# Norm, gate and last norm of batches 0 and 1 inside the last slots of attention 1; projections 0 and 1 back to back

## What is computed

```
x = x + L0_attn(norm(x))                 # 8 heads of 32, window 64
x = x + L0_xattn(ctx, norm(x))           # state space scan over ctx, gated by silu(norm(x))
x = x + L0_ffn(norm(x))                  # 256 -> 704 -> 256
x = x + L1_attn(norm(x))                 # 16 query heads of 128, 4 key/value heads, causal
x = x + L1_xattn(ctx, norm(x))           # second scan over ctx, gated by silu(norm(x))
x = x + L1_ffn(norm(x))                  # shared expert + 6 of 32 experts by a router

def L1_attn(x):                          # per batch
    q, k, v = split(x @ w_qkv.T)
    q, k = norm(q) * g + b, norm(k) * g + b      # per head
    q, k = rope(q), rope(k)
    return softmax(causal(q @ k.T / sqrt(128))) @ v @ w_o.T

def xattn(ctx, z):                       # u, delta, B, C come from ctx alone
    state[t] = state[t-1] * exp(delta[t] * A) + delta[t] * u[t] * B[t]
    return (state[t] @ C[t] + D * u[t]) * silu(z)
```

## Time and profile before

| | us |
|---|---|
| median of 3 runs | 902.63 (901.39 to 903.73) |
| the profiled execution | 903.65 |
| its span, first to last instruction | 901.9 |

### The profile page before, as it was taken

How to read it: one execution, slowest core, us unless ns; L and a number is a source line. 1 busy time by engine, 2 the same in 40 slices (tenths; PEclk the granted TensorE clock), 3 DMA queues, 4 the chain that set the end, 5 groups by cost and what they waited for, 6 DMA issues and landing times.

```text
span 901.9 us, 12578 instructions
## 1 busy us (share of the span) xinstructions
PE 747.9 (83%) x4016; PEld 576.4 (64%) x4016; DVE 688.0 (76%) x1230; ACT 490.2 (54%) x1062; POOL 352.6 (39%) x247
## 2 busy tenths in 40 slices
PE   6660479877799993699999999999856799999997
PEld 2240356554433573577877787878744689999996
DVE  4897689889879887798899899899967554444443
ACT  1744458640336602477786877788833354444442
POOL 1001355452331544223332423333533286666663
PEclk9885669898899997799999999999977899999999
DMA  4341124235020212011111111211400243444431
GB/s 173 122 154 42 70 93 140 96 140 221 1 76 0 59 59 93 0 48 36 48 45 38 48 48 36 60 36 51 151 1 0 100 147 136 142 139 143 139 132 47
DMA packets 28886, 74.66 MB, mean 83 GB/s; under 512 B 3632, under 2 KB 6336, under 8 KB 28448
## 3 DMA queue, kind: packets, MB, share of 16 engines
q1 hardware_dynamic: 28384, 71.51, 23.2%
q10 hardware_dynamic: 448, 2.49, 0.8%
HBM read 72.55 MB, written 1.44 MB: 82 GB/s over the span
## 4 chain that ended last, share of the span: by engine, by line
PE 54%; DVE 18%; issue 13%; ACT 11%; POOL 3%; DMA 1%; POOLq 0%; DVEq 0%; ACTq 0%; SPq 0%
PE ps L1864 6%; PE ps L1865 6%; PE ps L1866 6%; PE ps L1829 4%; PE ps L1706 4%; DVE hS L1033 3%; PE ps L1817 3%; PE ps L1752 2%; PE ps L1751 2%; PE ps L1750 2%; PE ps L1799 2%; PE ps L1798 2%; PE ps L1510 2%; DVE ps L1025 2%; PE ps L1483 1%
## 5 line engine op out<-in xcount | busy, mean ns | idle before, releaser
L420 POOL TENSOR_TENSOR hS<-hS,BCb 128x512 f32<-128x512 f32 x64 | 81.6, 1279 | 140.2 <-issue 69.0
L1462 DVE SCALAR_TENSOR_TENSOR arena<-ps,arena 128x1024 f32<-128x1024 f32 x32 | 39.2, 1225 | 101.6 <-ACT arena L899 93.1
L443 POOL TENSOR_TENSOR hS<-hS,BCb 128x1024 f32<-128x1024 f32 x23 | 56.1, 2440 | 108.2 <-DVE ps L1025 94.1
L509 POOL TENSOR_TENSOR MHl<-arena,MHh 128x1024 fp32r<-128x1024 f32 x34 | 81.8, 2405 | 17.2 <-ACT MHh L902 17.1
L1491 PE MATMUL ps<-ident,hS 128*128 128x128 f32 x256 | 40.7, 316 | 54.9 <-POOL hS L443 48.5
L1864 PE MATMUL ps<-Wh,MHh 128*128 128x256 f32 x272 | 77.8, 286 | 5.3 <-POOL MHl L509 5.3
L1063 DVE TENSOR_TENSOR_SCAN hS<-dA,ps 128x512 f32<-128x512 f32 x64 | 78.1, 1221 | 2.8 <-DVE ps L1054 0.6
L1866 PE MATMUL ps<-Wh,MHl 128*128 128x256 f32 x272 | 77.7, 286 | 0.0
L1865 PE MATMUL ps<-Wl,MHh 128*128 128x256 f32 x272 | 77.6, 285 | 0.0
L1491 PEld LDWEIGHTS ps<-ident,hS 128*128 128x128 f32 x256 | 33.7, 162 | 65.4 <-POOL hS L443 54.9
L506 POOL TENSOR_TENSOR Wl<-WB,Wh 128x512 fp32r<-128x512 f32 x34 | 47.1, 1388 | 64.5 <-ACT Wh L883 64.5
(11 more groups left out here) (241 smaller groups left out, 2100.7 us busy)
## 6 DMA issues: line engine op xcount, KB each, us to landing
BCb<-bc_dram SPq DMA_DIRECT2D x32, 512.0 KB, 3.5
BCb<-bcq_dram SPq DMA_DIRECT2D x64, 256.0 KB, 3.2
arena<-gate_dram SPq DMA_DIRECT2D x32, 512.0 KB, 3.8
WB<-in_we SPq DMA_DIRECT2D x34, 256.0 KB, 2.6
WB<-in_wqkv SPq DMA_DIRECT2D x1, 3072.0 KB, 12.7
WA<-in_wo ACTq DMA_DIRECT2D x1, 2048.0 KB, 7.9
WA<-in_ffn SPq DMA_DIRECT2D x1, 1408.0 KB, 7.9
pkb<-in_pk SPq DMA_DIRECT2D x2, 698.0 KB, 4.7
```

Source lines behind the costliest of these rows:

```text
L420: gp.tensor_tensor(h, h, qbc(q)[:, 1:2, :].broadcast_to([P, DT, S]), ALU.mult).then_inc(s["c_ready"], 1)
L443: gp.tensor_tensor(h, h, BCb[g % SB_LOADS][:, 1:2, :].broadcast_to([P, DT, HALF]), ALU.mult).then_inc(s["c_ready"], 1)
L509: gp.tensor_tensor(MHl[:, p, :], MH[p], MHh[:, p, :].bitcast(F32), ALU.subtract).then_inc(s["m_lo"], 1)
```

## The change

**End of attention 1.** Norm 4, gate and norm 5 of half 0, with transposes, copies, and the high and low parts of the result, become pieces of the plan in slots 53 to 63 (`GATE1_FIRST_HALF`). Behind the plan the same steps stand for half 1 alone. The tanh of layer 1 goes to the arena instead of `hT`. The low part of half 0 stays on VectorE, in slot 63. Counts on semaphores follow the new order (`ln_count`, `x_count`). The planner counts the new pieces of VectorE.

**Start of attention 1.** `ln_apply(3, 1)` becomes the piece `apply1`, behind `rope` of job 0 and job 1. Jobs 0 and 1 have `rope` three and `tr` four slots behind `proj` instead of two and three; the square of job 1 no longer waits for the sum of job 0. The transposes of half 1 (`ln1`) go from slot -6 to -3, V of batch 0 from -5 to -1 (behind the first scores). `accq` of quarters 6 to 9 goes behind projection 1. `da` of quarters 10 to 12 goes from slot 0 to -5. On GpSimd `w1_low(3)` and `(4)` stand ahead of `ln_rstd(3, (1,))` and `(5)` behind it, without the wait for norm 3.

```diff
+        gate_scratch = lambda l, hf: ar(4 + 8 * hf, 1024) if l else hT[:, hf, :]
...
+        def x_count(L, t):
+
+            if L == 4:
+                return XN_FFN + t // 2 + 1 + (t // 2 == B - 1)
+            if L == 5:
+                return XN_FFN + B + 2 * (t // 4)
+            return XN[L] - 1 + t // 4
+
+        LATE_LNS = {(4, 0): 8, (5, 0): 9, (4, 1): 10, (5, 1): 11}
+        ln_count = lambda L, hf: LATE_LNS.get((L, hf), 2 * L + hf) + 1
...
+            w1_low(3)
+            w1_low(4)
             ln_rstd(3, (1,))
-            pool.wait_ge(s["ln_h"], NT * 4)
-            w1_low(3)
+            w1_low(5)
...
-                elif kind == "sum":
+                if kind == "ln4":
+                    ln_rstd(4, (0,))
+                elif kind == "gate_x":
+                    ln_rstd(5, (0,))
+                elif kind == "sum":
                     job(JOB[a])
-                    if JOB[a] < 2:
-                        w1_low(4 + JOB[a])
...
-            ln_rstd(4)
+            ln_rstd(4, (1,))
...
-            ln_rstd(5)
+            ln_rstd(5, (1,))
...
-                if j:
+                if j >= 2:
                     act.wait_ge(s["job_sum"], j)
...
+            def final_high(hf):
+                act.wait_ge(s["ln_tr_dve"], 6 + hf + 1)
+                act.wait_ge(s["ln_tr_act"], 6 + hf + 1)
+                z = slice(512 * hf, 512 * hf + 512)
+                sc.copy(hTh[:, :, z], hT[:, :, z]).then_inc(s["h_hi"], 1)
...
+                if kind == "ln4_apply":
+                    gate_tanh(1, (0,))
+                elif kind == "ln5_copy":
+                    ln_tr_copy(3, (0,))
+                elif kind == "final":
+                    final_high(0)
...
-            ln_tr_copy(3)
+            ln_tr_copy(3, (1,))
+            final_high(1)
...
-            ln_apply(3, 1)
...
+            def final_low(hf):
+                z = slice(HALF * hf, HALF * hf + HALF)
+                dve.wait_ge(s["h_hi"], hf + 1)
+                v.tensor_tensor(hTl[:, :, z], hT[:, :, z], hTh[:, :, z].bitcast(F32), ALU.subtract).then_inc(s["h_lo_dve"], 1)
+
             for kind, a in ATT1_PLAN:
+                if kind == "ln4":
+                    ln_stats(4, 0)
+                elif kind == "ln4_apply":
+                    dve.wait_ge(s["job_mm"], len(JOB))
+                    dve.wait_ge(s["v_mm"], B)
+                    ln_apply(4, 0)
+                elif kind == "gate_h":
+                    gate_h(1, 0)
+                elif kind == "gate_x":
+                    gate_x(1, 0)
+                elif kind == "ln5_apply":
+                    ln_apply(5, 0)
+                elif kind == "ln5_copy":
+                    ln_tr_copy(3, 0)
+                elif kind == "final_low":
+                    final_low(0)
+                elif kind == "rot":
                     job(*a)
+                elif kind == "apply1":
+                    ln_apply(3, 1)
...
-            for hf in both:
-                ln_stats(4, hf)
-            dve.wait_ge(s["job_mm"], len(JOB))
-            dve.wait_ge(s["v_mm"], B)
-            for hf in both:
-                ln_apply(4, hf)
-            gate(1)
-            for hf in both:
-                ln_apply(5, hf)
-            for hf in both:
-                ln_tr_copy(3, hf)
...
+            ln_stats(4, 1)
+            ln_apply(4, 1)
+            gate_h(1, 1)
+            gate_x(1, 1)
+            ln_apply(5, 1)
+            ln_tr_copy(3, 1)
...
+            def gate_tr(l, halves=(0, 1)):
+
+                if l:
+                    pe.wait_ge(s["job_tr_copied"], 2 * len(JOB))
+                for hf in halves:
...
             fd(1)
-            for q in step:
-                accq(q)
             ln_ready(2, 0)
...
+                elif kind == "gate_tr":
+                    gate_tr(1, (0,))
+                elif kind == "ln5_tr":
+                    ln_tr(3, (0,))
+            gate_tr(1, (1,))
+            ln_tr(3, (1,))
...
+GATE1_FIRST_HALF = [(53, "ln4"), (54, "ln4_apply"), (55, "gate_h"), (56, "gate_tr"), (57, "gate_x"), (59, "ln5_apply"), (60, "ln5_tr"),
+                    (61, "ln5_copy"), (62, "final"), (63, "final_low")]
...
-    rope_job(-8, 0, 0, 2, 3)
-    rope_job(-7, 0, 1, 2, 3)
+    rope_job(-8, 0, 0, 3, 4)
+    rope_job(-7, 0, 1, 3, 4)
     at(-7, "wo1", 0)
-    at(-6, "ln1", 0)
-    v_job(-5, 0)
+    for q in range(Q_IN_FFN - 4, Q_IN_FFN):
+        at(-7, "acc", q)
+    at(-4, "apply1", 0)
+    at(-3, "ln1", 0)
+    v_job(-1, 0)
...
+    for slot, kind in GATE1_FIRST_HALF:
+        at(slot, kind, 0)
-    cost = {"rot": 2.6, "sum": 1.2, "rope": 3.2, "step": 2.0}
-    ssm = [("da", (m, d)) for m in range(Q_IN_FFN, Q_IN_FFN + 3) for d in range(DT)]
+    cost = {"ln4": 1.7, "ln4_apply": 1.4, "gate_h": 1.2, "gate_x": 4.3, "ln5_apply": 1.4, "ln5_copy": 0.7, "final_low": 1.2, "rot": 2.6, "sum": 1.2, "rope": 3.2, "step": 2.0}
+    ssm = []
+    for m in range(Q_IN_FFN, Q_IN_FFN + 3):
+        for d in range(DT):
+            at(-5, "da", (m, d))
...
-        plan += pick("ln1", "v", "proj") + behind
+        plan += pick("ln1", "v", "proj", "acc") + behind
...
-        plan += pick("vc", "sq")
+        plan += pick("vc", "sq", "da")
         if ok(u - 1):
             plan += [("pt", u - 1), ("ptc", u - 1)]
+        plan += pick(*(kind for _, kind in GATE1_FIRST_HALF))
         plan += [p for p in now if p[0] == "da"]
-        plan += pick("wo1", "rope", "rot", "sum")
+        plan += pick("wo1", "rope", "apply1", "rot", "sum")
```

More of the change, by code:

```diff
@@ L878, in _ @@
                     yq_copy(a)
-            gate_tanh(1)
+            gate_tanh(1, (1,))
             def w_high(x, src):
@@ L1245, in _ @@
+            for hf in both:
+                gate_h(0, hf)
+            for hf in both:
+                gate_x(0, hf)
             for hf in both:
@@ L1681, in _ @@
             acc_to(LAYER_STEPS - 1)
-            def gate_tr(l):
-                for hf in range(2):
+            def gate_tr(l, halves=(0, 1)):
+                if l:
+                    pe.wait_ge(s["job_tr_copied"], 2 * len(JOB))
+                for hf in halves:
                     pe.wait_ge(s["gate_h"], 2 * l + hf + 1)
```

76 lines of the change are left out of this document (29 added, 47 removed).

## The result

The changed kernel takes 904.75 us (median of 20 executions, 901.53 to 908.29) against 901.67 for the kernel before, measured beside it: a ratio of 1.0037, 95% interval 1.0025 to 1.0049. It is slower by 0.4%; the forecast was 0.6% faster. Its profiled execution took 905.45 us with a span of 903.7 us, 1.8 us more than the span of before.

What follows compares the result with a forecast made beforehand. Engines waiting on each other bound start and tail, nearly full TensorE and VectorE attention. 903.65 - 4.8 (tail) - 4.5 (start, net) + 3.5 (attention) = 897.85 profiled, 896.8 us median; range 890.5 to 904.

Steps and rivals of the forecast that it cites:

- Which views bound what: Attention 1 by stretches: engines wait for each other at start and tail; TensorE and VectorE nearly full in the early slots.
- The tail: Behind attention, to the router's end: half 1 goes through alone, 7.6 off the chain, 2.8 onto it, 4.8 us less.
- The start: From the feed-forward's last residual to the first `rc`: waiting falls from 15.2 to 6.3 us, 8.9 us shorter.
- What it pays there: Ahead of the start, GpSimd's `w1_low(3)` and `(4)` hold tiles 3 and 4 of `ln_apply(3, 0)`: 4.4 us later.
- Attention itself: Slots 0 to 63: half 0's work moves five scan steps into earlier slots, 3.5 us more, bounds 0 and 14.
- the lateness is nearly covered. I take a fifth: Early slots: ScalarE's own `da` work nearly covers VectorE's lateness, so 2 of 10.3 us of extra steps show.
- My 1.2: Last eleven slots: 11.5 us of moved pieces come in, 10.3 of steps leave, so 1.2 us more VectorE work.
- A: Rival at layer 3's norm tiles: they slip ahead of `w1_low` or TensorE has slack, 4.4 less, 892.4 us; chance 0.22.
- B: Rival in attention: VectorE becomes the bound and lateness isn't caught up, 14 us against 9.3 gained, 907.3 us; chance 0.10.
- C: Rival in attention: all 10.3 us of extra steps show but the rest doesn't, 903.6 us; chance 0.15.
- D: Rival at the start: it keeps its length as another wait replaces the one removed, 901.3 us; chance 0.10.
- Signs to look for: Changed profile: first `rc` about 370.3, residual 335, first to last `rc` 285, tail 23.6; wrong if `rc` stretch grows over 6.

Runs made afterwards that it cites:

- even: Kernel before plus a VectorE sum over 112 columns that nobody waits for in each of the 64 slots: 902.71 us, ratio 1.0003.
- start_only: Kernel before with only the part of the change ahead of attention 1: 898.42 us, ratio 0.9966.
- start_gated: Kernel before with the start part alone, plus a GpSimd wait for all four norm tiles ahead of `w1_low(3)`: 891.34 us, ratio 0.9886.
- end_only: Kernel before with only the change's part in and behind the last slots, planner costs included: 908.78 us, ratio 1.0072.
- steps_only: start_gated with scan steps placed as in the changed kernel (44 early, 10 late) and no piece moved: 898.48 us, ratio 0.9962.
- dve_only: start_gated plus five VectorE sums of 1.95 us in slots 5, 18, 24, 34 and 40: 894.98 us, ratio 0.9930.
- all_parts: start_gated plus five times a step's work on TensorE, VectorE, ScalarE and GpSimd, without moving batch boundaries: 895.61 us, ratio 0.9935.
- whole: Changed kernel with the GpSimd wait, 39 steps in their old slots and the five displaced ones whole in slots 5, 18, 24, 34, 40: 896.23 us, ratio 0.9938.
- y_behind_sq: Changed kernel with the GpSimd wait and ScalarE's copy of `y` put behind the square of its slot: 896.64 us, ratio 0.9932.
- whole_apart: whole with the copy of `y` last in its slot on ScalarE and the next batch's first accumulation one slot later: 895.61 us, ratio 0.9925.
- late_fixed: start_gated with half 0's norm 4 statistics, norm and tanh taken behind slot 63, GpSimd's 1/sqrt behind its last product with C: 892.07 us, ratio 0.9889.

## Why the prediction was wrong, point by point

- **Which views bound what**: right as read, wrong as used. TensorE at 227.84 and VectorE at 221.50 of 240.26 were both named as nearly full; I then priced VectorE's lateness alone.
- **The tail**, 4.8 less (bounds 4 to 5.5): 4.3 from the last residual to the router's end. Confirmed. The mis-sized term is the router: 5.29 instead of 4.79, at a granted clock of 0.67 instead of 0.74. I had reckoned with the last copy and not with the clock. Another 0.7 ahead of the last residual (5.91 instead of 6.64) can't be put down to the change: even, which leaves this place alone, has 5.91 too.
- **The start**, 8.9 shorter: 44.21 to 35.35, 8.86. Confirmed, in the changed kernel and in start_only (368.88 - 333.55 = 35.33). The waits came about as worked out, 1.10, 2.48 and 2.29 us on VectorE where I had 1.4, 2.4 and 2.5, and VectorE is busy 32.30 - 28.96 = 3.3 less, which are the two waits hidden in durations.
- **What it pays there**, 4.4 (bounds 0 to 4.9): the mechanism is confirmed by the fourth tile's 2.43 us and by start_gated, where one wait takes it away. The size was 5.5, outside the bounds. VectorE's tiles end 328.37 - 326.38 + 2.07 = 4.1 later, near the 4.5 worked out; the residual moves by 5.5, because TensorE, idle for 3.65 us, goes on at a granted clock of 0.69 instead of 1.00 and does its transposes and last tile in 5.55 us instead of 3.88. I had taken TensorE's queue as shifted rigidly. On the rule of "SBUF — State Buffer" of the Trainium skill, "Who interferes with whom", that the first to be issued keeps the ports: three tiles already queued did not stay ahead of GpSimd's instructions; they came through one for each end of a GpSimd instruction.
- **Attention itself**, 3.5 more (2 early, 1.5 late): this is the step that failed. It was 8.95 and 2.7, of which 1.7 go with the clock; without them the last eleven took 1.0 (end_only). The count of the steps was right (five, 39 to 44), and so was the direction. The sentence that failed is "the lateness is nearly covered. I take a fifth": five displaced steps cost 9 to 10 us in these slots, 4 to 5 times that (steps_only, 9.8). What was missing from the sum is that a step is four engines' work: on VectorE alone it costs 2.4 us for five (dve_only, near my 2), with TensorE's, ScalarE's and GpSimd's part 4.0 (all_parts), both at whole's places. And steps that come earlier move the handovers between two batches: in the changed kernel the copy of `y` lands where ScalarE has a square or a copy of V to do, and waits for TensorE ahead of it (1.7 us, y_behind_sq); in whole copy and first accumulation meet (2.3 us, whole_apart). The remaining 3 to 4 us of the 9.8 stay open, with ScalarE's larger part in the last chain as the only lead. The piece for the last eleven slots missed that five steps fewer give back 3.7 there and not 10.3, where TensorE is then busy 34.39 of 37.63 us (steps_only's window); and the pieces cost 4.7 and not 11.5. My 1.2 came out near the measured 1.0 because the two errors cancel, which is luck.
- **The rivals**. A, no block at the tiles: refuted, 6.36 us. B, slower: its sign, its point of decision (9.3 us between first and last `rc`, measured 11.65) and nearly its size came true, but not its mechanism: "VectorE becomes the bound" is refuted by even, 7.4 us more of VectorE's work for 0.6, and by the last chain of the changed kernel, which holds 0.1 us of VectorE in these slots. Its doubt, that a lateness isn't caught up, was the right one, and "where no projection runs VectorE makes up a late slot" was right for a lump of VectorE's work (1.0 us lost of 2.3) and wrong for a step. C, all 10.3 us show: its number for the early slots, 10.3, came near by accident, as five VectorE lumps of a step's length cost 2.4; so did its total, 903.6. D, start keeps its length: refuted.
- **Signs to look for**: `rc` first at 369.37 (370.3 forecast), residual at 334.02 (335), first to last `rc` 293.2 (285 forecast, over 291 for B), tail 24.0 (23.6). This execution was 2.1 us ahead at the scan, so counted from there the first two came at 371.4 and 336.1. "I am wrong if the stretch between the `rc` grows by over 6" is what happened.

## What to carry to other kernels

A planner that moves pieces from one full stretch into another trades on the cost of one engine; price a moved piece by all engines that it employs and by the handovers that its new place moves, and try the move alone, with nothing in the place that it leaves. Before a small gain is read from a profile, compare TensorE's granted clock over the same stretch: here it made 1.7 us of the loss in the last eleven slots, and took back the 0.9 us that late_fixed had gained. And before one engine's queue is moved forward, look what the other engine of a shared port is doing at that moment: one wait for its last tile was worth 6 us here.

## What was new about the hardware

- Of four queued tiles of VectorE beside GpSimd's instructions issued back to back, one came through at each of GpSimd's ends: four tiles that took 2.30 us with one of them held, and 1.38 with none (335.02 in the kernel before), took 6.36, and the fourth lasted 2.43 beside GpSimd's 2.39.
- TensorE, idle for 3.65 us behind these tiles, went on at a granted clock of 0.69, and twelve matmuls that took 2.95 us took 4.18. So the delay of the tiles, 4.1 us, reached their consumer as 5.5.
- In a ring of slots where TensorE is busy 95% and VectorE 92% of the time, 0.14 us more of VectorE's work in each slot cost 0.6 of 7.4 us, lumps of 2.3 us cost 1.0 each on average, and whole steps that employ four engines, moved in by the planner, cost 9.8 us for five, nearly their full length.
